# Spread GroupNorm statistics, an earlier normalise, later stores and ScalarE row copies in a two-layer convolution kernel

## The reference

```
x = x + conv0(groupnorm(x))        # 32 groups of 2 channels
x = x + conv1(sign(groupnorm(x)))
```

## Time and profile before

| what | value |
|---|---|
| median of 3 runs | 1866.14 us (1865.45 to 1870.02) |
| the profiled execution | 1866.56 us, its span 1864.8 us |
| PE busy | 1753.7 us, 94% of the span |
| DVE busy | 1683.8 us, 90% |
| ACT busy | 1078.4 us, 58% |
| POOL busy | 937.7 us, 50% |
| granted TensorE clock, mean | 0.994 |

### The profile page before, as it was taken

How to read it: one execution, slowest core, us unless ns; L and a number is a source line. 1 busy time by engine, 2 the same in 40 slices (tenths; PEclk the granted TensorE clock), 3 DMA queues, 4 the chain that set the end, 5 groups by cost and what they waited for, 6 DMA issues and landing times.

```text
span 1864.8 us, 75082 instructions
## 1 busy us (share of the span) xinstructions
PE 1753.7 (94%) x32458; PEld 1341.4 (72%) x32458; DVE 1683.8 (90%) x2525; ACT 1078.4 (58%) x1410; POOL 937.7 (50%) x702
## 2 busy tenths in 40 slices
PE   0499999999999999999999999999999999999997
PEld 0299996856565555765658999689986999766554
DVE  6789999999989999999999999999999999978886
ACT  2166665666556665666656666566655666566664
POOL 1255554555455554555545555455545555555552
PEclk9999999999999999999999999999999999999999
DMA  9758786777777776777767777677777777645554
GB/s 304 187 132 203 201 200 177 201 195 206 181 188 197 200 200 180 199 200 202 201 174 193 206 201 201 175 202 202 202 186 183 202 202 200 156 118 124 123 120 115
DMA packets 333993, 346.86 MB, mean 186 GB/s; under 512 B 27152, under 2 KB 301904, under 8 KB 333664
## 3 DMA queue, kind: packets, MB, share of 16 engines
q1 hardware_dynamic: 324768, 332.94, 69.7%
q10 hardware_dynamic: 8448, 8.39, 1.5%
q0 software_dynamic: 448, 0.73, 0.2%
HBM read 134.95 MB, written 134.22 MB: 144 GB/s over the span
## 4 chain that ended last, share of the span: by engine, by line
PE 82%; DVE 7%; DMA 5%; SPq 4%; issue 1%; ACT 1%; POOL 0%; DVEq 0%; ACTq 0%
PE psA L577 63%; PE psB L577 13%; PE psL L642 3%; DMA xh<-xn 3%; PE psA L662 3%; DMA ring<-in_x 2%; SPq L304 2%; SPq L287 2%; DVE bnt L822 1%; DVE ring L1039 1%; ACT xn L449 1%; DVE psL L1030 1%; DVE smalls L938 1%; DVE xc L994 1%; DVE ring L1014 1%
## 5 line engine op out<-in xcount | busy, mean ns | idle before, releaser
L577 PE MATMUL psA<-xh,W0h 64*64 64x512 f16 (+1 forms) x9216 | 982.5, 377 | 29.1 <-DMA xh<-xn 22.7
L577 PE MATMUL psA<-xl,W0h 64*64 64x512 f16 x9216 | 969.4, 378 | 0.0
L361 POOL TENSOR_TENSOR xl<-xc,xn 128x1024 f16<-128x1024 f32 (+2 forms) x347 | 586.5, 1703 | 663.7 <-ACT xn L449 652.5
L577 PEld LDWEIGHTS psA<-xl,W0h 64*64 64x64 f16 x9216 | 540.5, 107 | 121.6 <-issue 3.8
L577 PE MATMUL psA<-xh,W0l 64*64 64x512 f16 (+1 forms) x4704 | 617.2, 376 | 0.0
L577 PEld LDWEIGHTS psA<-xh,W0h 64*64 64x64 f16 x9216 | 518.0, 106 | 131.0 <-DMA xh<-xn 38.0
L577 PE MATMUL psB<-pk,W 64*64 64x512 f16 (+2 forms) x4944 | 602.0, 362 | 3.3 <-POOL pk L370 2.4
L467 ACT ACTIVATE sg<-ring,smalls 128x1024 f16<-128x1024 f32 (+2 forms) x270 | 297.6, 1107 | 267.7 <-DVE ring L1014 266.4
L370 POOL TENSOR_TENSOR pk<-pk,sg 128x520 f16<-128x520 f16 (+2 forms) x320 | 341.7, 1076 | 203.2 <-ACT pk L475 203.2
L1014 DVE SCALAR_TENSOR_TENSOR ring<-psA,smalls,ring 128x1024 f32<-128x1024 f32 x256 | 328.4, 1283 | 123.5 <-PE psA L662 123.4
L577 PEld LDWEIGHTS psB<-pk,W 64*64 64x64 f16 x4944 | 323.8, 107 | 83.9 <-POOL pk L370 4.0
(11 more groups left out here) (113 smaller groups left out, 892.5 us busy)
## 6 DMA issues: line engine op xcount, KB each, us to landing
out_y<-ring SPq DMA_DIRECT2D x512, 256.0 KB, 3.6
ring<-in_x SPq DMA_DIRECT2D x448, 256.0 KB, 4.0
xh<-xn SPq DMA_DIRECT2D x494, 129.0 KB, 2.8
ring<-in_x SPq DMA_DIRECT2D x16, 512.0 KB, 16.5
ring<-in_x ACTq DMA_DIRECT2D x16, 512.0 KB, 16.1
xh<-xn SPq DMA_DIRECT2D x180, 32.2 KB, 2.4
xh<-xn SPq DMA_DIRECT2D x16, 96.8 KB, 2.2
pk<-in_w1T POOLq DMA_DIRECT2D x2, 144.0 KB, 6.2
```

What stands on the lines that cost most here:

```text
L361: ins = nc.gpsimd.tensor_tensor(xl[:, slot:slot + rows, 1:W + 1], xc[:, j:j + rows], xn[:, k:k + rows, 1:W + 1], ALU.subtract)
L577: mm = pe.matmul(bank[out0:out0 + C, c0:c1], weights[src0:src0 + C, :], src[src0:src0 + C, slot:slot + rows, width[0]:width[0] + width[1]] ...
```

## The change

It has four parts.

1. **Statistics of the next image.** A new `join_tuples` at step 23 (`JOIN_STEP`) aggregates the tuples of the first 26 chunks (`JOINED`, 312 values) and writes the result back as one tuple, so that step 29 aggregates 75 values instead of 384. The edge-row ops of an image's first and last chunk leave `take_part` and run at steps 10 and 31; `border_of_group` moves from step 30 to step 31.
2. **Order of DVE.** `normalise(t+2)`, with its wait for `xl_rdy`, and `scale_of_group` move from the end of the step to directly behind `add_left`, ahead of `take_part` and `add_right`.
3. **Order of SP.** The store of step t is that of chunk t-5 instead of t-4, and stands between the swaps and the load.
4. **Single rows.** The one-row pieces of `xh` are no longer DMAs. ACT copies them from `xc`, with the halves exchanged, ahead of the `xn` activation of the same chunk (`singles`). The wait of ACT for the swaps at an image's second chunk goes with them.

```diff
-    def swaps(ch):
-        return ([(G * ch.z, 0, 1)] if ch.at(0) else []) + [(G * ch.z + 1, 1, shared(ch))] + again(ch)
+    def singles(ch):
+        return ([(G * ch.z, 0, 1)] if ch.at(0) else []) + again(ch)
...
+    JOIN_STEP, AGGR_STEP, SCALE_STEP = NC - 9, NC - 3, NC - 2
+    JOINED = JOIN_STEP + BEFORE - NC + 1
...
                 for (i0, i1), (o0, o1) in ((LO, HI), (HI, LO)):
-                    for slot, j, rows in swaps(ch):
-                        k = buf(ch, j)
-                        sp.dma_start(xh[o0:o1, slot:slot + rows, :],
-                                     xn[i0:i1, k:k + rows, :]).then_inc(xh_in[n % 2], 16)
+                    sp.dma_start(xh[o0:o1, lo:lo + rows, :],
+                                 xn[i0:i1, k:k + rows, :]).then_inc(xh_in[n % 2], 16)
...
                 if t + 1 < ALL:
                     swap_high(t + 1)
+                if t > LAG + 1:
+                    store_chunk(t - LAG - 2)
                 if RING <= t + RING - LAG - 3 < ALL:
                     load_chunk(t + RING - LAG - 3)
-                if t > LAG:
-                    store_chunk(t - LAG - 1)
...
-                if n > 1 and ch.at(1):
-                    act.wait_ge(xh_in[0], xh_count(n - 1))
+                for (i0, i1), (o0, o1) in ((LO, HI), (HI, LO)):
+                    for slot, j, rows in singles(ch):
+                        nc.scalar.activation(xh[o0:o1, slot:slot + rows, 1:W + 1], xc[i0:i1, j:j + rows], ACT.Copy)
...
+            def join_tuples(img):
+                steps = Steps(stats_chain, STATS_STEPS, img)
+                dve.wait_ge(bn_done, (img - 1) * NC + JOINED)
+                steps.link(nc.vector.bn_aggr(aggr, first_tuples))
+                nc.vector.memset(joined[:, 0:1], float(JOINED * CE))
+                nc.vector.tensor_copy(joined[:, 1:2], aggr[:, 0:1])
+                steps.link(nc.vector.tensor_scalar(joined[:, 2:3], aggr[:, 1:2], float(JOINED * CE), None, ALU.mult))
...
-                steps.link(nc.vector.bn_aggr(aggr, bnt[:].rearrange("p n s -> p (n s)")))
+                steps.link(nc.vector.bn_aggr(aggr, last_tuples if img > 0 else flat))
...
                 if t > LAG:
                     add_left(*of(t - LAG - 1))
+                if scaling:
+                    scale_of_group(img + 1)
+                if t + 2 < ALL:
+                    dve.wait_ge(xl_rdy, t + 2)
+                    normalise(*of(t + 2))
                 for g in parts_at(t):
                     if g < ALL:
                         take_part(g)
                 if t > LAG:
                     add_right(*of(t - LAG - 1))
                 if img + 1 < NB:
-                    if a == AGGR_STEP:
+                    if a == 10:
+                        edge_row(img + 1, 0)
+                    elif a == JOIN_STEP:
+                        join_tuples(img + 1)
+                    elif a == AGGR_STEP:
                         stats_parts(img + 1)
-                    elif a == SCALE_STEP:
-                        scale_of_group(img + 1)
-                if t + 2 < ALL:
-                    dve.wait_ge(xl_rdy, t + 2)
-                    normalise(*of(t + 2))
-                if a == SCALE_STEP and img + 1 < NB:
-                    border_of_group(img + 1)
+                    elif a == NC - 1:
+                        edge_row(img + 1, NC - 1).then_inc(edge_rdy, 1)
+                        dve.wait_ge(edge_rdy, img + 1)
+                        border_of_group(img + 1)
```

More of the change, by code:

```diff
@@ L102, in together @@
         return [(0, 0, G + 1)] if ch.at(0) else kept(ch) + again(ch)
-    def swaps(ch):
-        return ([(G * ch.z, 0, 1)] if ch.at(0) else []) + [(G * ch.z + 1, 1, shared(ch))] + again(ch)
+    def singles(ch):
+        return ([(G * ch.z, 0, 1)] if ch.at(0) else []) + again(ch)
     def xh_count(n):
-        return 32 * sum(len(swaps(Chunk(m))) for m in range(n % 2, n + 1, 2) if m > 0)
+        return 32 * (n // 2 if n % 2 == 0 else n // 2 + 1)
     def buf(ch, j):
@@ L125, in parts_at @@
         return range(NC, NC + 3) if t == 0 else range(t + BEFORE, t + BEFORE + 1)
-    AGGR_STEP, SCALE_STEP = NC - 3, NC - 2
+    JOIN_STEP, AGGR_STEP, SCALE_STEP = NC - 9, NC - 3, NC - 2
+    JOINED = JOIN_STEP + BEFORE - NC + 1
     with ExitStack() as ctx:
@@ L234, in conv_preact @@
         border_rdy = sem("border_ready")
+        edge_rdy = sem("edge_row_ready")
         prep_done = sem("preparation_done")
@@ L283, in swap_high @@
                     sp.wait_ge(products_done, n - 1)
+                k, lo, rows = buf(ch, 1), G * ch.z + 1, shared(ch)
                 for (i0, i1), (o0, o1) in ((LO, HI), (HI, LO)):
-                    for slot, j, rows in swaps(ch):
-                        k = buf(ch, j)
-                        sp.dma_start(xh[o0:o1, slot:slot + rows, :],
-                                     xn[i0:i1, k:k + rows, :]).then_inc(xh_in[n % 2], 16)
+                    sp.dma_start(xh[o0:o1, lo:lo + rows, :],
+                                 xn[i0:i1, k:k + rows, :]).then_inc(xh_in[n % 2], 16)
             def store_chunk(g):
@@ L314, in _ @@
                     swap_high(t + 1)
+                if t > LAG + 1:
+                    store_chunk(t - LAG - 2)
                 if RING <= t + RING - LAG - 3 < ALL:
                     load_chunk(t + RING - LAG - 3)
-                if t > LAG:
-                    store_chunk(t - LAG - 1)
-            for g in range(ALL - LAG - 1, ALL):
+            for g in range(ALL - LAG - 2, ALL):
                 store_chunk(g)
@@ L834, in take_borders, with edge_row @@
                 if img > 0:
-                    ins = nc.vector.reduce_sum(colp[:, :, i], edge_columns(at, G), AX.X)
+                    return nc.vector.reduce_sum(colp[:, :, i], edge_columns(at, G), AX.X)
+                return edge_row(img, i) or ins
+            def edge_row(img, i):
+                at, ins = place(img, i), None
                 for edge, (p0, p1), lo in ((0, LO, at), (NC - 1, HI, at + CE - W)):
@@ L922, in link @@
                     dve.wait_ge(self.sem, self.count)
-            STATS_STEPS = 10
+            STATS_STEPS = 12
             def take_part(g):
@@ L931, in take_part @@
                 take_borders(img, i).then_inc(bn_done, 1)
+            flat = bnt[:].rearrange("p n s -> p (n s)")
+            cut = 12 * JOINED
+            first_tuples, joined, last_tuples = flat[:, 0:cut], flat[:, cut - 3:cut], flat[:, cut - 3:12 * NC]
+            def join_tuples(img):
[5 more added lines that the diff above has]
+                steps.link(nc.vector.tensor_scalar(joined[:, 2:3], aggr[:, 1:2], float(JOINED * CE), None, ALU.mult))
             def stats_parts(img):
-                steps = Steps(stats_chain, STATS_STEPS, img)
+                steps = Steps(stats_chain, STATS_STEPS, img, 2)
                 if img > 0:
@@ L946, in stats_of_group @@
                 dve.wait_ge(gath_rdy, img + 1)
-                steps = Steps(stats_chain, STATS_STEPS, img, 1)
+                steps = Steps(stats_chain, STATS_STEPS, img, 3)
                 nc.vector.reduce_sum(st[:, 3:4], psL[:, 0, 4:8], AX.X)
@@ L959, in scale_of_group @@
             def scale_of_group(img):
-                steps = Steps(stats_chain, STATS_STEPS, img, 4)
+                steps = Steps(stats_chain, STATS_STEPS, img, 6)
                 dve.wait_ge(xc_rdy, img * NC)
@@ L975, in border_of_group @@
             def border_of_group(img):
-                steps = Steps(stats_chain, STATS_STEPS, img, 9)
+                steps = Steps(stats_chain, STATS_STEPS, img, 11)
                 steps.link(nc.vector.scalar_tensor_tensor(out=parts6[:, 0, :], in0=counts, scalar=mean0[:, 0:1],
@@ L1046, in _ @@
             link(ins)
+            spare_steps = Steps(stats_chain, STATS_STEPS, 0)
+            spare_steps.link(nc.vector.memset(spare[:], 0.0))
+            spare_steps.link(nc.vector.memset(spare[:], 0.0))
             stats_parts(0)
@@ L1070, in _ @@
                     add_layer0(*of(t - 1))
-                if a == SCALE_STEP and img + 1 < NB:
+                scaling = a == SCALE_STEP and img + 1 < NB
+                if scaling:
                     stats_of_group(img + 1)
```

1 line of the change is left out of this document (removed).

## The result

| | before | changed |
|---|---|---|
| median | 1865.8 us (1861.43 to 1870.02, 4 runs) | 2109.61 us (2106.62 to 2112.26, 4 runs) |
| span of the profiled execution | 1864.8 us | 2107.4 us |
| PE busy | 94% | 86% |
| DVE busy | 90% | 83% |
| mean granted TensorE clock | 0.994 | 0.982 |

The changed kernel takes 1.1307 times as long (95% interval 1.1276 to 1.1337): 244 us slower, where 266 were forecast.

What follows compares the result with a forecast made beforehand. PE was taken to bound the kernel at 6.71 us a step; a new loop of 6.92 + 0.75 + 0.42 = 8.09 over 214 steps adds 295 us, less 27 won back, net 268 on 1866.6, rounded to 2132 us (range 2080 to 2180).

Steps and rivals of the forecast that it cites:

- The loop: Right addition, rounding, `xn`, `xl`, normalise, statistics, right addition: closed once a step, 6.92 us against PE's 6.71.
- rounding to `xn`: 0.80: Loop term on ACT: 0.80 us from the rounding to `xn` of the next chunk.
- the first rival: Loop without the collision: pack and normalise do not meet, a step is 7.34 us, total 1974 us; chance 0.20.
- (2 x 6.71 + 8.17) / 3: First rival's variant: plain steps keep PE's pace, only z = 2 pays; 7.20 us a step, 1944 us total.
- The collision: Normalise on DVE meets POOL's pack and is delayed, 0.75 us a step on average, bounds 0 and 0.95.
- the 0.2 us computed: Computed margin between the starts of pack and normalise, cited for the rival of a loop without collision.
- Single rows: Two ACT copies at z = 2 add 0.60 us, `xl` 0.65: 1.25 every third step, 0.42 on average.
- 8.09: Forecast step in us: loop 6.92, collision 0.75 and single rows 0.42, 1.38 more than 6.71.
- Loads don't wait: Stores on SP: a store lands within one step, so the later store does not delay loads through ring slots.
- The price of the short aggregation: DVE's statistics aggregation at step 29, 1.88 us before, was taken as 0.5 us after the change.
- 295 us for 214 steps at 1.38, less 27: Forecast sum: 295 us of longer steps, less 10 us of late swaps and 17 us of image changes.
- The stalls that could be won back: PE's stalls, 44 us: about 34 at seven image changes, perhaps 10 from late swaps elsewhere.

Runs made afterwards that it cites:

- experiment 4: Changed kernel with the rounding moved behind the next `xn` in ACT's queue: 1921.7 us, 1.0282 of the kernel before.
- experiment 1: Changed kernel with the normalise and scale operations put back behind the right addition, other three parts kept: 1858.86 us, 0.9953 of the kernel before.
- (2): Kernel before with only the normalise and scale operations moved behind the left addition: 2031.35 us, 1.0875 of the kernel before.
- experiment 3: Changed kernel with one more wait, POOL's pack waiting for the normalise of its step: 1958.51 us, 1.0492 of the kernel before.
- experiment 6: Changed kernel with rounding behind the next `xn` on ACT and POOL's pack waiting for the normalise: 1850.61 us, 0.9912 of the kernel before.

## Why the prediction was right, point by point

- **The loop.** Right in its members and in its effect. Loosening one link (experiment 4), or undoing the move itself (1), removes most or all of the cost; making the move alone (2) costs 163.5 us. The term "rounding to `xn`: 0.80" was mis-sized: in the loop `xn` follows after 0.58. The row that it came from could have said so: there the normalise ended at 156.44 + 0.80 = 157.24, later than 156.62 + 0.58 = 157.20, so `xn` was not ready to run behind the rounding. The plain loop is 6.66, not 6.92, and so just below PE's step. Plain steps without collision cost nothing: the variant of the first rival, "(2 x 6.71 + 8.17) / 3" = 7.20, describes experiment 3 better than the 7.34 beside it (7.26 measured away from the image changes).
- **The collision.** Right, and it decides more than the plain loop does. Predicted 0.75 on average; the step lasts 7.93 with it and 7.26 without, 0.67. The margin that the first rival rested on was thinner than the 0.2 us computed: in the first step shown the pack's input is done at 410.56 (409.92 + 0.64 in ACT's timeline) and `xl` at 410.53. The normalise was delayed even so in 170 of 195 steps; where the pack came later, as in the last step shown, it is short.
- **Single rows.** Predicted 0.60 per z = 2 chunk from the 1.36 us of a pair of `xn` pieces; it is 1.00, because two 64x256 copies take 0.85 together and the first starts 0.72 behind the rounding, where `xn` starts 0.58 behind it. With the second `xl` (0.64, predicted 0.65) the term is 0.55 a step instead of 0.42. The measured terms add up to 6.66 + 0.67 + 0.55 = 7.88, near the 7.93 found. That the forecast's 8.09 lies only 0.16 above is in part luck: the loop was taken 0.26 too long and the collision 0.08, the single rows 0.13 too short.
- **Stores.** "Loads don't wait" looked at the slot of the ring alone, and there it was right. But the load stood last in SP's order, and where PE leads DVE waited 81.0 us for it (experiment 1). In the changed kernel itself, where a step is 1.2 us longer, the wait for loads is 15.7 us as before, so the number was not touched.
- **Statistics.** The price of the short aggregation was right (0.48 for 0.5). Alone, this part brings 12 us.
- **Total.** 295 us for 214 steps at 1.38, less 27, was forecast; that sum is 268 us, which gives 2134 rather than the 2132 written. Measured against 6.71, 211 steps at 7.93 make 257 us more. The stalls that could be won back in these steps were 44 us in the kernel before, as forecast, but split otherwise: 39 around the six image changes and 4 elsewhere. In the changed kernel 19 us of them are left, so 25 came back where 27 were forecast. That leaves 233 us for these steps, and about 10 us lie before the fifth and behind the 216th rounding. So the length of the step made the forecast too high, 295 against 257, and the 10 us at both ends, which it did not price, hid a part of that.
- **The skill's rule.** The Trainium skill (SBUF — State Buffer, Who interferes with whom) says that the loser blocks fully for the other's instruction, and that issue order decides who blocks. The trace agrees that one waits for the other, and in one clear case on the order: with the pack 0.16 us behind, the normalise keeps its 0.81 and the pack takes 1.68. Where the normalise loses, it ends less than its own 0.80 after the pack (410.57 + 1.79 is 0.55 behind 410.64 + 1.17), so a literal full block would overstate it by 0.25 us. The normalise of 410.57 starts 0.07 us ahead of the pack and still is the one that waits, so starts that lie this close don't tell the order of issue.

## What to carry to other kernels

Before moving a wait ahead of other work on an engine, write down who is released by that work and follow the releases until they return to the wait; add up the durations and compare the sum with the step of the bounding engine. The busy shares give no hint, and an undisturbed step in the old trace, in which the moved wait would have been nil, misleads. If the early position is wanted all the same, take one link out of the cycle by reordering another engine's queue, and let the operation off the critical path wait, so that it doesn't delay the one on it: the two together turned 244 us of loss into 17 us of gain.

## What the runs showed of the hardware

In most steps of the changed kernel the pack starts 0.02 to 0.10 us ahead of the normalise and delays it. A pack that starts up to 0.08 us behind the normalise still delays it (410.57 and 410.64 above); from 0.14 us on it waits itself (427.30 and 427.46). At 0.10 us both outcomes occur, with 1 us of DVE time at stake:

```profile
781.66 1.82 DVE L1012 TENSOR_SCALAR xc<-ring,smalls 128x1024 f32<-128x1024 f32 x1 [0.51 <-POOL xl L362]
781.76 1.17 POOL L371 TENSOR_TENSOR pk<-pk,sg 128x520 f16<-128x520 f16 x1
...
1554.53 0.81 DVE L1012 TENSOR_SCALAR xc<-ring,smalls 128x1024 f32<-128x1024 f32 x1 [0.50 <-POOL xl L362]
1554.63 1.74 POOL L371 TENSOR_TENSOR pk<-pk,sg 128x520 f16<-128x520 f16 x1
```

The granted clock fell in more places than before: its mean is 0.982 against 0.994. Cut into windows of 75 us between the start and the last image, the changed kernel has it below 1.00 in 11 of 22 windows, the kernel before in 4 of 20. Around the second image change of the changed kernel PE is busy for 1.27 of 4 us, and in the 5 us behind that the granted clock is 0.50, which is 1.2 GHz; 1.00 is 2.4 GHz. The rows are us from and to, length, busy us of PE, PEld, DVE, ACT and POOL, granted clock, DMA share and GB/s:

```profile
560.00:575.00 15.00, 11.00 (x161) 5.32 (x157) 12.25 (x31) 6.08 (x10) 7.04 (x6) 0.77 0.67 171
562.00:566.00 4.00, 1.27 (x20) 0.50 (x20) 3.25 (x7) 0.27 (x1) 2.29 (x4) 0.87 0.93 226
566.00:571.00 5.00, 4.12 (x38) 2.13 (x42) 4.82 (x16) 2.73 (x5) 1.58 (x1) 0.50 0.53 131
```

How much of the 244 us this adds was not measured by itself; with loop and collision removed (experiment 6) the mean clock is back at 0.995.
